# Cross-attention over 32 batches: another order of TensorE's units, of the other engines' steps and of the transfers

## The reference

```python
qp = (q @ Wq.T + bq).reshape(b, t_q, h, d // h).transpose(0, 2, 1, 3)
kp = (k @ Wk.T + bk).reshape(b, t_kv, h, d // h).transpose(0, 2, 1, 3)
vp = (v @ Wv.T + bv).reshape(b, t_kv, h, d // h).transpose(0, 2, 1, 3)
scores = jnp.einsum('bhqd,bhkd->bhqk', qp, kp) / jnp.sqrt(jnp.float32(d))
scores = jnp.where(mask, -jnp.inf, scores)
attn = jax.nn.softmax(scores, axis=-1)
out = jnp.einsum('bhqk,bhkd->bhqd', attn, vp)
...
x = x + _L0_xattn_ref(_layernorm(x, axis=-1), ctx_1024, ctx_1024, mask_BxSxS2_ik1, ...)
x = x + _L0_attn_ref(_layernorm(x, axis=-1), ...)
x = x + _L0_ffn_ref(_layernorm(x, axis=-1), ...)
```

## Time and profile before

| | |
|---|---|
| median of 3 runs | 1944.77 us (1942.69 to 1945.35) |
| the profiled execution | 1940.98 us |
| its span in the trace | 1939.2 us |
| busy in the span: PE, PEld, DVE, ACT, POOL | 90%, 60%, 71%, 67%, 67% |
| granted TensorE clock over the span | 0.94 |
| the 32 periods of the cross-attention | from 66.8 to 1413.5 us |

### The profile page before, as it was taken

The page is one execution under the profiler, slowest core; times in us unless marked ns, Lnnn a source line. Parts: engine busy times, 40 slices in busy tenths (PEclk is TensorE's granted clock), DMA queues, the critical chain, the costliest instruction groups (busy, mean ns, idle before and its releaser), DMA issues. The chain is left out here.

```text
span 1939.2 us, 59104 instructions
## 1 busy us (share of the span) xinstructions
PE 1749.3 (90%) x24652; PEld 1155.3 (60%) x24673; DVE 1384.8 (71%) x3589; ACT 1298.0 (67%) x1595; POOL 1293.0 (67%) x669
## 2 busy tenths in 40 slices
PE   3789999999999999999999999999867886599996
PEld 1346666666666666666666666666533565488885
DVE  5568888888888888788888888888467576644442
ACT  2258788887888888888878888788745543133332
POOL 1248888988888888888888888888733200244432
PEclk9779999999999999999999999999778786699998
DMA  4444445444455454544445544444156675588884
GB/s 152 167 107 116 125 135 141 126 113 129 117 154 132 109 130 114 154 130 116 123 119 153 138 112 119 123 136 107 28 170 215 200 264 191 194 250 267 248 248 126
DMA packets 169867, 290.83 MB, mean 150 GB/s; under 512 B 56450, under 2 KB 136706, under 8 KB 169442
## 3 DMA queue, kind: packets, MB, share of 16 engines
q1 hardware_dynamic: 162114, 276.83, 49.0%
q0 software_dynamic: 7488, 10.23, 2.6%
HBM read 169.80 MB, written 33.16 MB: 105 GB/s over the span
## 5 line engine op out<-in xcount | busy, mean ns | idle before, releaser
L405 POOL TENSOR_TENSOR pl<-pT,ph 128x1024 f16<-128x1024 f32 x416 | 882.0, 2133 | 182.4 <-ACT ph L641 182.3
L535 DVE CUSTOM_DVE_ANT_0 junk<-ring,mbias 128x804 bf16<-128x804 f32 x512 | 507.3, 991 | 170.4 <-issue 159.8
L639 ACT ACTIVATE pT<-score,lift 128x1024 f32<-128x1024 f32 (+1 forms) x416 | 464.5, 1117 | 75.0 <-PE o_acc L769 38.0
L641 ACT ACTIVATE ph<-score,lift 128x1024 f16<-128x1024 f32 (+1 forms) x416 | 464.3, 1116 | 0.0
L708 PE MATMUL ring<-wvp,cp 128*128 128x256 f16 (+1 forms) x2496 | 311.2, 276 | 4.4 <-DVE kl L498 0.5
L696 PE MATMUL ring<-cp,wkp 128*128 128x402 f16 x1536 | 307.6, 337 | 5.2 <-DVE kst L464 1.8
L708 PEld LDWEIGHTS ring<-wvp,cp 128*128 128x128 f16 (+1 forms) x2496 | 236.4, 100 | 82.3 <-issue 50.0
L399 POOL TENSOR_TENSOR cp<-cx,cp 128x804 f16<-128x804 f32 x128 | 252.4, 1992 | 49.3 <-ACT cp L599 49.3
L723 PE MATMUL ring<-kh,qm 32*128 32x402 f16 x1024 | 265.2, 338 | 19.6 <-DVE mx L535 10.2
L628 ACT ACTIVATE kh<-ring,bks 128x402 f16<-128x402 f32 x256 | 155.2, 606 | 174.7 <-PE ring L696 174.7
L769 PE MATMUL o_acc<-v,pl 128*128 128x33 f16 (+1 forms) x3328 | 242.6, 179 | 0.1
(11 more groups left out here) (232 smaller groups left out, 2055.1 us busy)
## 6 DMA issues: line engine op xcount, KB each, us to landing
cx<-in_ctxT SPq DMA_DIRECT2D x32, 1601.0 KB
w1p<-wsp SPq DMA_DIRECT2D x24, 1408.0 KB, 8.2
kst<-kh SPq DMA_DIRECT2D x256, 100.5 KB, 2.9
msk<-in_mask SPq DMA_DIRECT2D x64, 400.2 KB, 5.5
kst<-kh SPq DMA_DIRECT2D x256, 99.6 KB, 2.5
wsp<-w_parts SPq DMA_DIRECT2D x24, 704.0 KB, 4.3
w2p<-wsp SPq DMA_DIRECT2D x24, 640.0 KB
kst<-kl SPq DMA_DIRECT2D x128, 100.5 KB, 2.7
```

The source lines that it names most:

```text
L405: pool.tensor_tensor(pl[:, u].rearrange("p h q -> p (h q)"), pT[:, u], ph[:, u].rearrange("p h q -> p (h q)"), ALU.subtract).then_inc(pl_r ...
L535: dve.tensor_tensor_reduce(junk[:, n % 2], ring[:, 0:2, 0:KW], mbias[:, j, 2 * KW * half:2 * KW * half + 2 * KW].rearrange("p (c k) -> p c ...
L639: act.activation(pT[0:n, u].rearrange("k (h a q) -> k a h q", a=2, q=S), scored, ACT.Exp, bias=lift[0:n, 0:1], scale=SSCALE)
L641: act.activation(ph[0:n, u].rearrange("k h (a q) -> k a h q", a=2), scored, ACT.Exp, bias=lift[0:n, 0:1], scale=SSCALE).then_inc(exp_done, 1)
```

## The change

The five tables are written anew: TensorE's units are in another order, with 44 instead of 48 changes of array tiling per period (counted around the period's end, T's two included); ACT, POOL and DVE get orders to match; V5, V6 and T change places in the ring (V5 from bank 0 to 1, V6 from 1 to 0, T from 1 to 0). SP's steps get a table of their own. In it only one thing is changed: the shift rows are issued ahead of the second half of the stacked keys, no longer behind it. No instruction is added, removed or resized. From line 95 on, the new file counts one line more, behind SP's period five more (`MP` is L565, `SPR` L556, `SH` L550).

```diff
-PE_ORDER = steps("K0 S0 K1 S1 K2 V0 K3 S2 K4 M0 S3 W0 M1 S4 W1 M2 V1 M3 W2 W3 S5 M4 K5 M5 S6 S7 M6 V2 W4 M7 W5 S8 M8 K6 "
-                 "M9 W6 S9 M10 K7 M11 S10 W7 M12 W8 S11 M13 V3 M14 S12 W9 W10 M15 V4 W11 T V5 V6 W12")
-ACT_ORDER = steps("KH0 E0 KH1 KH2 E1 KH3 E2 KH4 E3 E4 CH0 E5 KH5 CH1 E6 E7 E8 KH6 CH2 E9 KH7 E10 CH3 E11 E12")
...
+PE_ORDER = steps("K0 S0 S1 K1 K2 V0 K3 W0 S2 S3 M0 K4 M1 W1 S4 M2 V1 M3 W2 S5 S6 M4 K5 M5 W3 W4 M6 V2 M7 W5 S7 S8 M8 K6 "
+                 "M9 W6 S9 M10 K7 M11 W7 S10 M12 V3 M13 S11 W8 M14 S12 W9 M15 W10 V4 T V5 W11 V6 W12")
+ACT_ORDER = steps("KH0 E0 KH1 KH2 E1 KH3 E2 KH4 E3 E4 E5 KH5 CH0 E6 CH1 CH2 CH3 E7 KH6 E8 KH7 E9 E10 E11 E12")
...
+SP_ORDER = steps("CTX QST STKA MASK QM SHIFT STKB")
+K_BANK, V_BANK, T_BANK = (2, 1, 2, 1, 2, 2, 2, 2), (0, 2, 2, 2, 2, 1, 0), 0
...
                     def period(b, i, j, do_a, do_b):
-                        if has_later(b):
-                            load_context(b + 2)
...
-                        if do_b:
-                            stack_keys(b + 1, 1 - j, 1)
-                            shift_queries(b + 1, 1 - j)
+                        for kind, n in SP_ORDER:
...
+                            elif kind == "STKB" and do_b:
+                                stack_keys(b + 1, 1 - j, 1)
+                            elif kind == "SHIFT" and do_b:
+                                shift_queries(b + 1, 1 - j)
```

More of the change, by code:

```diff
@@ L86, in steps @@
     return [(w.rstrip("0123456789"), int("0" + w.lstrip("ABCDEFGHIJKLMNOPQRSTUVWXYZ"))) for w in text.split()]
-PE_ORDER = steps("K0 S0 K1 S1 K2 V0 K3 S2 K4 M0 S3 W0 M1 S4 W1 M2 V1 M3 W2 W3 S5 M4 K5 M5 S6 S7 M6 V2 W4 M7 W5 S8 M8 K6 "
-                 "M9 W6 S9 M10 K7 M11 S10 W7 M12 W8 S11 M13 V3 M14 S12 W9 W10 M15 V4 W11 T V5 V6 W12")
-ACT_ORDER = steps("KH0 E0 KH1 KH2 E1 KH3 E2 KH4 E3 E4 CH0 E5 KH5 CH1 E6 E7 E8 KH6 CH2 E9 KH7 E10 CH3 E11 E12")
[L92 to L95, removed]
+PE_ORDER = steps("K0 S0 S1 K1 K2 V0 K3 W0 S2 S3 M0 K4 M1 W1 S4 M2 V1 M3 W2 S5 S6 M4 K5 M5 W3 W4 M6 V2 M7 W5 S7 S8 M8 K6 "
+                 "M9 W6 S9 M10 K7 M11 W7 S10 M12 V3 M13 S11 W8 M14 S12 W9 M15 W10 V4 T V5 W11 V6 W12")
+ACT_ORDER = steps("KH0 E0 KH1 KH2 E1 KH3 E2 KH4 E3 E4 E5 KH5 CH0 E6 CH1 CH2 CH3 E7 KH6 E8 KH7 E9 E10 E11 E12")
+POOL_ORDER = steps("L0 L1 L2 L3 L4 L5 ADD L6 CL0 L7 L8 L9 L10 L11 L12 CL1 CL2 CL3")
+DVE_ORDER = steps("KL0 N KL1 KL2 VH0 VL0 KL3 X0 X1 KL4 X2 VH1 X3 VL1 X4 X5 KL5 X6 VH2 X7 VL2 X8 X9 KL6 X10 X11 KL7 X12 "
+                  "X13 VH3 X14 VL3 X15 SH MP SPR VH4 VL4 VH5 VH6 VL5 VL6")
+SP_ORDER = steps("CTX QST STKA MASK QM SHIFT STKB")
+K_BANK, V_BANK, T_BANK = (2, 1, 2, 1, 2, 2, 2, 2), (0, 2, 2, 2, 2, 1, 0), 0
 BANK = {("K", n): bank for n, bank in enumerate(K_BANK)} | {("V", n): bank for n, bank in enumerate(V_BANK)} | {("T", 0): T_BANK}
@@ L357, in period @@
                     def period(b, i, j, do_a, do_b):
-                        if has_later(b):
-                            load_context(b + 2)
-                        if do_b:
[L361 to L366, removed]
-                            stack_keys(b + 1, 1 - j, 1)
-                            shift_queries(b + 1, 1 - j)
+                        for kind, n in SP_ORDER:
+                            if kind == "CTX" and has_later(b):
+                                load_context(b + 2)
+                            elif kind == "QST" and do_b:
+                                stack_queries(b + 1, 1 - j)
+                            elif kind == "STKA" and do_b:
+                                stack_keys(b + 1, 1 - j, 0)
+                            elif kind == "MASK" and has_later(b):
+                                load_mask(b + 2)
+                            elif kind == "QM" and has_later(b):
+                                load_block_queries(b + 2, j)
+                            elif kind == "STKB" and do_b:
+                                stack_keys(b + 1, 1 - j, 1)
+                            elif kind == "SHIFT" and do_b:
+                                shift_queries(b + 1, 1 - j)
                     shift_rows = a["shift_row"][0:PAIRS * NK].partition_broadcast(STRIP)
```

## The result

The changed kernel takes 1955.43 us (median of 4 runs, 1955.16 to 1957.39), the kernel before beside it 1944.55 (1942.69 to 1945.35). The ratio is 1.006, its 95% interval 1.0042 to 1.0077: slower by 0.6%, or 10.9 us, where 12.9 were forecast. The profiled execution is the one of 1955.43 us, with a span of 1953.6.

What follows compares the result with a forecast made beforehand. TensorE's own order was taken to bound the kernel, with waits on other engines. Unit order -0.08, MP +0.75 less 0.02, shift rows -0.22 gave +0.43 per period, 30 times +12.9 us: 1957.7 us; range 1935 to 1970.

Steps and rivals of the forecast that it cites:

- MP beside L11 and L12: At the period's end: MP waits for L11's end, L12 ends 0.75 us late, W12 and the next K0 follow.
- the sum: Per period: -0.08 unit order, +0.75 less 0.02 slack for MP, -0.22 shift rows; +0.43, times 30 = +12.9 us.
- rival 1: MP halts the running L for its full price, L12 1.15 us late: +0.83 per period, 1969 us; chance 0.12.
- rival 3: MP loses against L12 too, V6 waits for SPR: +1.8 us per period, 1999 us; chance 0.05.
- The price: L12's delay from MP: 0.98 less 0.25, say 0.75 us; bounds nothing and 1.15 us.
- The order of the units: TensorE's order: four changes of tiling fewer, 0.36 us per period, mostly lost to waits; counted as -0.08 us.
- the walk: TensorE's new order followed unit by unit with three wait rules: period 40.4 us if nothing else binds.
- The shift rows: SP's order: shift rows issued ahead of 12 stacking DMAs end late S0s; counted as -0.22 us per period.

## Why the prediction was right, and where its steps were not

**MP beside L11 and L12: right, in mechanism and size.** It was said that MP waits from 36.9 to 37.7 and runs to 38.6, that L12 takes 2.9 and W12 starts at 40.65; measured were 36.85, 37.70, 38.55, 2.88 and 40.59. With MP cut to 2 columns the period is 40.32 instead of 41.07: the 0.75 us of the sum, without any cover. The bounds have been seen too: rival 1's 1.15 us is what MP costs a CL that starts 0.32 ahead of it, and rival 3 is the kernel with MP early in the old order, where the wait was right and the clock came on top. The price was taken from rows 10, two back-to-back POOL steps with a waiting VectorE step between them, and that was the right row to take. One reading of this part was a little off: before, L12 ended at 564.66, 0.48 us ahead of W12 and not well over half a microsecond; nothing in the sum hangs on it.

The Trainium skill (SBUF — State Buffer, Who interferes with whom) says that whoever issues first gets the shared port pair for its whole instruction. L11, and L12 in the kernel with MP early, agree: MP waited 0.85 and 2.04 us for them. The CL of the kernel before does not fit by the starts in the trace, and the one beside 2 columns, at the same distance, fits again. No run here shows issue times of VectorE apart from the start of its rows.

**The order of the units: right in kind, too small.** K3 at 5.84, W0 at 6.87, W8 at 32.62 (said: 32.67), E11 at 33.37 (33.4), M15 at 34.85 (34.9) and V6 at 39.29 (39.3) are the walk's. M0 came at 8.54 and not 8.44: it takes bank 1, where K3's result still waits for KL3, which the walk left out. Later waits were shorter by about as much. Without MP the period is 40.32, where the walk had 40.40; against the usual period of before (40.49) the order brings 0.17 us, twice the 0.08 of the sum. With the mask on ScalarE in both orders it is 0.15.

**The shift rows: the size was right by luck, the step was wrong.** The sum took 0.22 us per period for SP's order, since the shift rows "stood behind 12 stacking DMAs". They did in the program, but in time the DMAs were mostly out before SPR ended: they account for 1.4 of the 6.8 us by which S0 was late over all periods, or 0.05 us per period. The changed kernel with SP's old order shows that with the new order nothing hangs on the transfers: by the prediction's step it should have taken 0.22 x 30 = 6.6 us more than the changed kernel, and its ratio is the same (1.0062 and 1.0060). What went is nearly all of the 0.2 us between mean and usual period (40.70 and 40.49 before, 41.10 and 41.07 after). Part of it went because S0 is 0.3 us further from SPR, by W11's place behind T; that covers most of the four late issues, and takes 0.3 us off each slow landing. The rest went because the trace after has three slow landings where the one before has six, and that is not explained. The rows that tell the two apart are the end of SPR beside the issue of the shift rows.

**The sum.** Per usual period it is -0.17 and +0.75, and the longer periods give back 0.18: 0.40, as by T, against 0.43 in the forecast. The forecast was 2.3 us high in time. That it is so close is in part luck, since the order brought 0.09 more than its term, and the shift rows 0.04 less for another reason than the one given. Of the difference between the two profiled executions, 14.4 us of span, 12.3 lie between the first and the last T (1274.1 - 1261.8). The rest is 0.9 us less ahead of the first T, 1.7 more from the last T to the end of the stage, and 1.4 more behind the stage, where both programs are the same. The medians of the runs differ by less, 10.9 us, so a microsecond or two of it can't be put down to anything.

**What stays open.** Why 2 columns wait for a CL where 800 stop it; and why some landings are slow, and fewer of them after. The first is not needed for the result; the second is behind most of the 0.18 us that the longer periods gave back.

## What to carry to other kernels

When a VectorE step and a GpSimd step exclude each other, ask not whether they overlap but which GpSimd step comes behind, and what waits for that one: a loss of 1.15 us on a CL cost nothing, one of 0.75 on another CL cost 0.4, and one of 0.75 on L12 its full size, and moving the step to a third engine made it free. A tighter order of the bounding engine takes away cover that others lived on, so a side effect that was free before has to be priced anew in it. Before a late transfer is put down to the queue, compare its issue with the end of what it waits for, in each late period and not in one. And when the bounding engine has to stand still for some 2 us, read its granted clock behind that wait: here the wait of 2.19 us cost 1.42 us more by the clock.

## What the runs showed of the hardware

- A GpSimd step that loses to a VectorE step loses the time from its own start to the other's end, less 0.15 us, in all the periods of six such meetings; it can thus lose more (1.15 us) than the VectorE step takes (0.98).
- A VectorE step of 2 columns waits for a running L just as one of 1601 does (0.88 us in all), and for a CL (1.42 us in all) that one of 800 or 1601 stops.
- Where TensorE stood still for 2.19 us once per period, its granted clock was at the 1.2 GHz level for a stretch of nearly every period (0.51 from 601.60 to 605.10), and the first six matmuls of the next period took 2.05 us instead of 1.18. In the kernel before, where the longest wait between 200 and 1000 us is the 0.88 us of the earlier trace rows, the clock stayed at 1.00 for those 800 us.
- A second wait ahead of X0, a VectorE step on the critical cycle, cost 0.14 us per period.
- The slow landings of the shift rows come at regular distances. In the changed kernel the three late ones are at 485, 855 and 1226 us:

```profile
L356 SPq DMA_DIRECT2D qst<-turned x1: 524/524/524, 485.0 to 485.0; - x1
...
DMA to landing us min/median/max: 3.2/3.2/3.2
```

```profile
L356 SPq DMA_DIRECT2D qst<-turned x1: 508/508/508, 854.9 to 854.9; - x1
...
DMA to landing us min/median/max: 3.6/3.6/3.6
```

  Before, they are at 441 and 483, 808 and 849, and 1174 and 1215 us. The distance of some 370 us is the same in both; what causes it was not tried.
